# One opening stage for modulation, projections and rates, and a second queue for the first recurrent weights

## The chip, the cores and the metric

The kernel runs on one core of one Trainium2 chip. Its time is the device time of one execution in microseconds (us); less is better. The engines are named as in the profile: PE (TensorE matmul), PEld (its weight load), DVE (VectorE), ACT (ScalarE), POOL (GpSimd) and SP (SyncE, which here only issues transfers). SPq marks an instruction of SP's queue that issues a transfer.

## The reference

A transformer block with conditioned normalisation, a recurrent attention layer with fast weights, and a mixture of experts. The change touches the opening of it:

```
mod = (silu(c) @ wmod).reshape(16, 6, 1, 256)
sa, ca, ga, sb, cb, gb = (mod[:, j] for j in range(6))
ga, gb = (2 * (g >= 0) - 1) * max(abs(g), 0.25)
h   = layernorm(x) * (1 + ca) + sa              # x: (16, 256, 256)
qkv = silu(h @ W_qkv)                            # W_qkv: (256, 768); q and k scaled to length 1
lr  = softplus(h @ W_lr + b_lr + const)          # W_lr: (256, 6)
...                                              # recurrent stage over chunks of 64 tokens, w0, w1, w2
x = x + ga * attention
h = layernorm(x) * (1 + cb) + sb
x = x + gb * experts(h)                          # 64 experts, 6 for each token
```

## The kernel before

The program is a row of stages, each a block in which every engine has its own instruction list, with semaphores between them. A stage ends with a barrier of all engines (`PhaseSems.__exit__`, L65 and L66), before which SP waits for every store of the stage. The stages that matter here:

- `phase_modulation` (L118 to L187). SP loads `ct` (c transposed, 16 KB) and the whole of `wmod` (`wm`, 1536 KB). ACT and DVE make silu(c) out of Exp, add, reciprocal and multiply. PE makes all 1536 columns as 16 rows (a batch each), DVE copies them out of PSUM, adds 1 to the two scales and bounds the two gates, each step waiting for the one before. The table goes to DRAM (`scratch_mod`).
- `phase_qkv` (L190 to L450). 16 batches (b) of 256 tokens, two halves (u) of 128. A step s runs from -1 to 19; in it DVE has the statistics of batch s+1, ACT and PE the projection of batch s-1, DVE the lengths of q and k of batch s-2, PE and ACT the transposition of batch s-3 (`turn_y`, `keep_y`). `turn_h` transposes a normalised batch into `psH`; `keep_h` (ACT) copies it with the batch's scale and shift as per-partition operands, from `modT`, which is `scratch_mod` read back and transposed by PE. `qkv` makes 774 columns in `psQ`; `silu` (ACT) and `rates` (DVE, L393) empty it. `store_kv` and `store_t` write to DRAM, and so does a store of the 6 unfinished rates of each token (`scratch_zlr`). `psT` serves both `turn_y` and, ahead of the loop, the transposed modulation.
- `phase_rates` (L453 to L485). Reads `scratch_zlr` as 128 x 192, does softplus with Exp and Ln (another table of ACT), and writes `scratch_lr`.
- `phase_fast_weights` (from L560). The recurrent stage: two streams x of 16 iterations. PE and DVE both begin with `wait_ge(preload, 192)`, which is 12 loads of 128 KB: `firstT` (6, the weights transposed) and `first` (6). All are on SP's queue: `firstT`, then `load_kv(0, 0)` (4 of `kvT`, 2 of `kv`, 2 of `lr`), then `first`. Behind these stand `load_kv(1, 0)`, `wproj`, `onorm`, `wgate`. DVE, before its first piece of the recurrence, sums the squares of `firstT` (L1124, L1127), scales `wproj` (L1320), and adds to `code` (L1323), which POOL makes after the roots of those sums (L1346).
- The later stages (routing, experts, combination) read `scratch_mod` for the gate, at another index after the change, and are otherwise the same.

The order on each engine is the order of the code; nothing reorders it.

## Time and profile before

| | us |
|---|---|
| median of 3 runs | 1862.06 (1853.25 to 1863.24) |
| the profiled execution, its own time | 1872.18 |
| its span, first to last instruction | 1870.4 |
| PE busy | 1605.9 (86% of the span) |
| DVE busy | 1176.2 (63%) |
| ACT busy | 884.2 (47%) |
| POOL busy | 783.5 (42%) |
| modulation stage, to the first instruction of the next | 0 to 25.35 |
| projection stage | 25.35 to 164.51 |
| rates stage | 164.51 to 170.97 |

A busy share is a mean over the whole span. The stages follow each other with a barrier between them, so the time of a short stage is read from its own stretch of the trace, where the engines are mostly idle, and not from the shares.

### The profile page before, as it was taken

The page shows a single profiled execution, that of the slowest core. Times are in us where ns is not written, and L with a number is a line of the kernel's source. Part 1 is how long each engine was busy: PE and PEld are TensorE (multiplying, and loading weights), DVE is VectorE, ACT ScalarE, POOL GpSimd, SP SyncE. Part 2 cuts the span into 40 slices and gives each one's busy share as a digit, 9 for nine tenths or more (in the row PEclk, how much of TensorE's full clock was granted, in tenths as well). Part 3 has the DMA queues.
Part 4 walks back from the last instruction along what each step waited for, and adds up shares of the span by engine and source line. Part 5 has one row for each costly group of instructions (what it writes and reads, how often), then busy time and mean ns, then how long its engine had stood idle before and what let it go on. Part 6 is the DMA issues. An engine that isn't in the chain of part 4 may idle for free. (4 is left out here: it accounts for less than half of the span.)

```text
span 1870.4 us, 41123 instructions
## 1 busy us (share of the span) xinstructions
PE 1605.9 (86%) x11163; PEld 1197.3 (64%) x11227; DVE 1176.2 (63%) x4255; ACT 884.2 (47%) x2156; POOL 783.5 (42%) x818
## 2 busy tenths in 40 slices
PE   3993799888888888898872499999999999998996
PEld 1662577666666676666651377777777777776764
DVE  2662578878887778888873454444444444443877
ACT  1773377656566666666650133333333333332221
POOL 0331233455455545555567133333333333342333
PEclk7996799989998989999995699999999999999999
DMA  2675444444444442223223455555555556323997
GB/s 87 186 213 170 118 138 129 129 146 141 128 139 136 146 129 81 78 82 95 67 80 120 128 161 160 166 160 167 159 157 167 153 166 202 95 57 74 266 269 191
DMA packets 264288, 263.54 MB, mean 141 GB/s; under 512 B 87931, under 2 KB 235880, under 8 KB 264080
## 3 DMA queue, kind: packets, MB, share of 16 engines
q1 hardware_dynamic: 200592, 170.98, 32.1%
q0 software_dynamic: 21504, 51.18, 7.7%
q10 hardware_dynamic: 41984, 38.82, 7.6%
q8 instruction: 105, 1.72, 0.4%
q14 instruction: 103, 0.84, 0.2%
HBM read 141.91 MB, written 127.31 MB: 144 GB/s over the span
## 5 line engine op out<-in xcount | busy, mean ns | idle before, releaser
L1728 POOL DMA_INDIRECT scratch_y<-e_eo,e_goes x256 | 250.4, 978 | 408.8 <-ACT e_eo L1818 349.4
L1754 PE MATMUL e_psGU<-wgu,e_xT 128*128 x1024 | 352.1, 466 | 4.9 <-ACT e_xT L1811 2.7
L1862 DVE COPY e_hT<-e_psH 88x256 f32<-88x256 f32 x256 | 107.7, 421 | 338.3 <-PE e_psH L1763 257.5
L1770 PE MATMUL e_psD<-wd,e_hT 88*128 x1024 | 263.8, 380 | 0.0
L1754 PEld LDWEIGHTS e_psGU<-wgu,e_xT 128*128 128x128 f32 x1024 | 183.8, 190 | 92.6 <-issue 24.9
L1392 POOL DMA_INDIRECT scratch_buf<-rows,dest x192 | 192.0, 1000 | 49.1 <-issue 48.9
L1402 POOL TENSOR_TENSOR f_wnr<-f_wss,f_half 128x4 f32<-128x4 f32 x96 | 99.8, 1040 | 266.9 <-DVE f_wss L1212 265.0
L1807 ACT ACTIVATE e_sgm<-e_psGU 128x176 f32<-128x176 f32 x256 | 81.2, 317 | 239.5 <-PE e_psGU L1754 200.7
L1770 PEld LDWEIGHTS e_psD<-wd,e_hT 88*128 88x128 f32 x1024 | 174.1, 190 | 14.1 <-issue 0.4
L1818 ACT ACTIVATE e_eo<-e_psD 128x256 f32<-128x256 f32 x256 | 98.1, 383 | 159.0 <-issue 93.3
L1740 PEld LDWEIGHTS e_psX<-ident,e_xg 128*128 128x128 f32 x512 | 72.3, 141 | 73.1 <-issue 39.6
L1740 PE MATMUL e_psX<-ident,e_xg 128*128 128x128 f32 x512 | 98.3, 274 | 6.1 <-DMA e_xg<-scratch_buf 6.1
L1811 ACT ACTIVATE e_xT<-e_psX 128x256 f32<-128x256 f32 x256 | 97.2, 380 | 6.2 <-issue 5.7
L1048 ACT ACTIVATE f_wsq<-f_WT 128x512 f32<-128x512 f32 x96 | 60.5, 630 | 83.7 <-DVE f_WT L1208 76.6
L889 PE MATMUL prod<-f_A,f_beta_i 128*128 128x512 bf16 x192 | 74.8, 390 | 20.7 <-DVE f_A L1199 14.1
L891 PEld LDWEIGHTS prod<-f_A 128*128 128x128 bf16 x768 | 60.5, 100 | 47.9 <-issue 4.4
L1016 ACT ACTIVATE f_X<-spare 128x512 bf16<-128x512 f32 x96 | 57.4, 598 | 71.1 <-PE spare L908 71.1
L322 PE MATMUL q_psQ<-q_wq,q_hT 128*128 128x512 f32 (+1 forms) x256 | 90.5, 498 | 0.0
L1884 DVE TENSOR_TENSOR e_hh<-e_psGU,e_sgm 128x176 f32<-128x176 f32 x256 | 84.8, 331 | 5.7 <-ACT e_sgm L1807 5.6
L2051 DVE SCALAR_TENSOR_TENSOR c_acc<-c_g,wk,c_acc 128x256 f32<-128x256 f32 x160 | 78.6, 491 | 5.7
L1397 POOL TENSOR_TENSOR f_nb<-f_ssb,f_half 128x12 bf16<-128x12 bf16 x32 | 72.5, 2264 | 13.6 <-DVE f_ssb L1184 13.1
L891 PE MATMUL prod<-f_A 128*128 128x128 bf16 x768 | 76.0, 223 | 0.0
(305 smaller groups left out, 3779.3 us busy)
## 6 DMA issues: line engine op xcount, KB each, us to landing
e_xg<-scratch_buf ACTq DMA_DIRECT2D x256, 132.0 KB
scratch_y<-f_blank SPq DMA_DIRECT2D x64, 384.0 KB
c_g<-scratch_y SPq DMA_DIRECT2D x64, 384.0 KB, 12.0
scratch_qkvT<-q_tT SPq DMA_DIRECT2D x16, 768.0 KB
wgu<-in_wgT SPq DMA_DIRECT2D x64, 176.0 KB
wgu<-in_wuT SPq DMA_DIRECT2D x64, 176.0 KB
wd<-in_wdT SPq DMA_DIRECT2D x64, 176.0 KB
scratch_buf<-f_blank SPq DMA_DIRECT2D x65, 132.0 KB, 2.2
```

Source lines behind the costliest of these rows:

```text
L322: mm = pe.matmul(psQ[:, u, lo:hi], hT[:, b % 2, k, u, :], wq[:, k, lo:hi], start=(k == 0), stop=(k == KD - 1))
L891: mm = pe.matmul(dst[:, q, :], a[:, x, m, q, :], a[:, x, m, q, :], start=False, stop=(q == Q - 1))
L1392: pool.indirect_dma_start(out=T["buf"], out_offset=bass.IndirectOffsetOnAxis(dest[:, i, k:k + 1], 0), in_=rows[:, i % RR, :], in_offset=No ...
L1402: pool.tensor_tensor(wnr[:, x, cols], wss[:, x, cols], half[:, 0:Q], ALU.pow).then_inc(wn1[x].sem, 1)
L1728: pool.indirect_dma_start(out=T["y"], out_offset=bass.IndirectOffsetOnAxis(goes[:, n:n + 1], 0), in_=eo[:, n % OB, :], in_offset=None, bou ...
L1740: mm = pe.transpose(psX[:, j % 2, k * P:(k + 1) * P], xg[j % GB][:, k * P:(k + 1) * P], ident[:, :])
L1754: mm = pe.matmul(psGU[:, j % 2, 0:2 * F], xT[:, j % 2, k, :], wgu[:, bass.ds(buf, 1), k, :].rearrange("p b n -> p (b n)"), start=(k == 0), ...
L1770: mm = pe.matmul(psD[:, j % 2, 0:D], hT[0:FH, j % 2, k, :], wd[0:FH, buf, k, :].rearrange("p b n -> p (b n)"), start=(k == 0), stop=(k == 1))
L1811: act.activation(xT[:, j % 2, :, :].rearrange("p k t -> p (k t)"), psX[:, j % 2, 0:KD * P], ACT.Copy).then_inc(xd, 1)
L1818: act.activation(eo[:, b % OB, :], psD[:, b % 2, 0:D], ACT.Copy).then_inc(eod, 1)
L1862: v.tensor_copy(hT[0:FH, b, :, :].rearrange("p k t -> p (k t)"), psH[0:FH, b, 0:2 * P]).then_inc(htd, 1)
L1884: v.tensor_tensor(hh[:, b, :], psGU[:, b, F:2 * F], sgm[:, b, :], ALU.mult).then_inc(hd, 1)
```

## The change

Three things. First, `phase_modulation` and `phase_rates` are gone and their work stands in `phase_qkv`. The shift and scale of the first normalisation are made by PE directly as columns (`modT`, channels on partitions) from the first 512 columns of `wmod`; ACT's Silu makes silu(c). The other four rows are made after step 2 (`other_columns` on PE, `others` on DVE) in `psT`, which PE must not use again until DVE has copied it (`pe.wait_ge(n_kept, 1)`), and stored at step 4. Secondly, the rates stay in SBUF (`zl`, 128 x 32 x 6); softplus is done in the last steps, and `scratch_lr` has another layout: (128, 32, 6), so that a chunk's 64 tokens are 64 rows of 24 bytes, 768 bytes apart, where they were adjacent. The 16 stores of `scratch_zlr` are gone. Thirdly, in the recurrent stage the six loads of `first` are issued by ACT, and `firstT` stands on SP's queue behind `load_kv(0, 0)`.

```diff
-def phase_modulation(nc, T):
...
-def phase_rates(nc, T):
...
 def phase_qkv(nc, T):
@@ sync
-            load(0)
-            sp.dma_start(mod[:, :], T["mod"][:, 0:2, :].rearrange("b j d -> b (j d)")).then_inc(m_in, 16)
+            wv = T["wmod"].rearrange("(k p) n -> p k n", p=P)
+            sp.dma_start(ct[:, :].rearrange("p (k b) -> p k b", k=KD),
+                         T["cT"].rearrange("(k p) b -> p k b", p=P)).then_inc(c_in, 16)
+            load(0)
+            sp.dma_start(wm[:, :, 0:2 * D], wv[:, :, 0:2 * D]).then_inc(m_in, 16)
             sp.dma_start(wq[:, :, 0:3 * D], T["wqkv"].rearrange("(k p) n -> p k n", p=P)).then_inc(wload, 16)
             sp.dma_start(wq[:, :, 3 * D:NQ], T["wlr"].rearrange("(k p) n -> p k n", p=P)).then_inc(wload, 16)
+            load(1)
             sp.dma_start(blr[:, :], T["blr"].rearrange("(a n) -> a n", a=1).broadcast_to([P, NLR])).then_inc(wload, 16)
-            for b in range(1, NX):
+            load(2)
+            sp.dma_start(wm[:, :, 2 * D:6 * D], wv[:, :, 2 * D:6 * D]).then_inc(n_in, 16)
+            for b in range(3, NX):
                 load(b)
...
+            sp.wait_ge(lr_d, 1)
+            sp.dma_start(T["lr"].rearrange("p t n -> p (t n)"), lr[:, :, :].rearrange("p t n -> p (t n)")).then_inc(lr_out, 16)
@@ tensor
+            def other_columns():
+                pe.wait_ge(n_in, 16)
+                for n in range(2):
+                    for k in range(KD):
+                        mm = pe.matmul(psT[0:B, n * 512:(n + 1) * 512], ct[:, k * B:(k + 1) * B],
+                                       wm[:, k, 2 * D + n * 512:2 * D + (n + 1) * 512], start=(k == 0), stop=(k == KD - 1))
+                mm.then_inc(n_made, 1)
...
+            pe.wait_ge(c_silu, 1)
             pe.wait_ge(m_in, 16)
             for j in range(2 * KD):
-                mm = pe.transpose(psT[:, j * B:(j + 1) * B], mod[:, j * P:(j + 1) * P], ident[0:B, 0:B])
-            mm.then_inc(m_turned, 1)
-            pe.wait_ge(m_kept, 1)
-            pe.wait_ge(wload, 48)
+                for k in range(KD):
+                    mm = pe.matmul(psT[:, j * B:(j + 1) * B], wm[:, k, j * P:(j + 1) * P], ct[:, k * B:(k + 1) * B],
+                                   start=(k == 0), stop=(k == KD - 1))
+            mm.then_inc(m_made, 1)
+            pe.wait_ge(id_done, 2)
...
+                if s == 2:
+                    pe.wait_ge(m_kept, 2)
+                    other_columns()
+                    pe.wait_ge(n_kept, 1)
@@ scalar, after the halves of step s
+                if s == B:
+                    act.preload_act_table_set("natural_log_exp_and_others")
+                    act.wait_ge(neg_d, 1)
+                    act.activation(low[:, :, :], low[:, :, :], ACT.Exp).then_inc(exp_d, 1)
+                    act.wait_ge(exp_d, 1)
+                    act.activation(low[:, :, :], low[:, :, :], ACT.Ln, bias=1.0).then_inc(ln_d, 1)
@@ vector
-            v.wait_ge(wload, 48)
             for s in steps:
+                if s == 1:
+                    v.wait_ge(wload, 48)
                 if real(s - 2):
                     rates(s - 2, 1)
+                if s == B + 1:
+                    v.wait_ge(zl_d, B * UPB)
+                    v.scalar_tensor_tensor(out=low[:, :, :], in0=zl[:, :, :], scalar=-1.0, in1=zl[:, :, :],
+                                           op0=ALU.mult, op1=ALU.min).then_inc(neg_d, 1)
...
                 if real(s - 1):
                     rates(s - 1, 0)
+                if s == 2:
+                    others()
+            v.wait_ge(ln_d, 1)
+            v.scalar_tensor_tensor(out=lr[:, :, :], in0=zl[:, :, :], scalar=0.0, in1=low[:, :, :],
+                                   op0=ALU.max, op1=ALU.add).then_inc(lr_d, 1)
 def phase_fast_weights:
-        lrv = T["lr"].rearrange("(g x s c t) n -> x s g c t n", g=NG, x=2, s=2, c=NC)
+        lrv = T["lr"].rearrange("(h t) (g x s u) n -> x s g u h t n", t=CH, g=NG, x=2, s=2)
@@ sync
-            for w, n in enumerate(names):
-                for b2 in range(2):
-                    sp.dma_start(firstT[:, w, 2 * b2:2 * b2 + 2, :], T[n + "T"].rearrange("h p n -> p h n")).then_inc(preload, 16)
...
             load_kv(0, 0)
             for w, n in enumerate(names):
                 for b2 in range(2):
-                    sp.dma_start(first[:, w, 2 * b2:2 * b2 + 2, :], T[n].rearrange("h p n -> p h n")).then_inc(preload, 16)
+                    sp.dma_start(firstT[:, w, 2 * b2:2 * b2 + 2, :], T[n + "T"].rearrange("h p n -> p h n")).then_inc(preload, 16)
             load_kv(1, 0)
@@ scalar
+            for w, n in enumerate(names):
+                for b2 in range(2):
+                    act.dma_start(first[:, w, 2 * b2:2 * b2 + 2, :], T[n].rearrange("h p n -> p h n")).then_inc(preload, 16)
             act.preload_act_table_set(ACT_SET)
```

`others` does to the four rows on DVE what `phase_modulation` did to six: the copy out of PSUM (16 x 1024 where it was 16 x 1536), the added 1 (one row now), and the six steps of the gates on 16 x 512, each waiting for the one before.

How the lists move at three places. SP's list from the start of the program, before:

```order
L142 DMA m_ct<-in_cT 128x2x16
L144 DMA m_wm<-in_wmod 128x2x1536
L146 DMA scratch_mod<-m_mod 16x1536
L120 UNCONDITIONAL_BRANCH
L244 UNCONDITIONAL_BRANCH
L249 DMA q_x<-in_x 128x2x256
L266 DMA q_mod<-scratch_mod 16x512
L267 DMA q_wq<-in_wqkv 128x2x768
L268 DMA q_wq<-in_wlr 128x2x6
L269 DMA q_blr<-in_blr 128x6
```

and of the change:

```order
L198 DMA q_ct<-in_cT 128x2x16
L184 DMA q_x<-in_x 128x2x256
L201 DMA q_wm<-in_wmod 128x2x512
L202 DMA q_wq<-in_wqkv 128x2x768
L203 DMA q_wq<-in_wlr 128x2x6
L184 DMA q_x<-in_x 128x2x256
L205 DMA q_blr<-in_blr 128x6
L184 DMA q_x<-in_x 128x2x256
L207 DMA q_wm<-in_wmod 128x2x1024
```

The store of the table, the barrier (the two branches) and the read back are gone; the second batch of x stands between the two small loads, behind 512 KB of `wm` and 768 KB of `wq`.

PE's list at the end of step 2 and in step 3, of the change (before, the same without the row of L277):

```order
L269 MATMUL q_psQ<-q_wq,q_hT 128x262 x2
L277 MATMUL q_psT<-q_wm,q_ct 16x512 x4
L251 MATMUL q_psH<-q_ident,q_xn 128x128 x4
L258 MATMUL q_psT<-q_ident,q_y 128x128 x6
L269 MATMUL q_psQ<-q_wq,q_hT 128x512 x2
L269 MATMUL q_psQ<-q_wq,q_hT 128x262 x2
```

Four matmuls of 512 columns stand between the last projection of batch 1 and `turn_h(3)`, and `turn_h(3)` also waits for DVE's copy.

ACT's list at the end of the projections, of the change (before, the four `keep_y` of the row L317 follow the square at once, and the table load, Exp and Ln stand behind a barrier):

```order
L331 ACTIVATE q_sq<-q_y 128x512
L351 ACT_TABLE_LOAD
L353 ACTIVATE q_low<-q_low 128x192
L355 ACTIVATE q_low<-q_low 128x192
L317 ACTIVATE q_tT<-q_psT 128x6x128 x4
L123 UNCONDITIONAL_BRANCH
L972 UNCONDITIONAL_BRANCH
L1073 DMA f_first<-in_w 128x2x128 x6
L1074 ACT_TABLE_LOAD
```

The softplus moved ahead of the last four copies, and ACT begins the recurrent stage with six issues.

## Rows read from the trace of the kernel before

**Rows 1.** The page, part 1: busy us, share, instructions.

```profile
PE 1605.9 (86%) x11163; PEld 1197.3 (64%) x11227; DVE 1176.2 (63%) x4255; ACT 884.2 (47%) x2156; POOL 783.5 (42%) x818
```

**Rows 2.** Busy time by stretch: engines, granted clock, DMA share, GB/s.

```profile
0.00:25.35 25.35, 7.27 (x12) 1.31 (x12) 5.91 (x11) 1.51 (x2) 0.20 (x4) 0.90 0.23 67
25.35:39.55 14.20, 2.58 (x13) 2.13 (x14) 4.59 (x19) 2.53 (x4) 2.01 (x6) 0.50 0.56 169
60.00:150.00 90.00, 90.00 (x415) 60.58 (x414) 58.91 (x181) 66.54 (x102) 28.52 (x24) 1.00 0.72 218
164.51:170.97 6.46, 0.00 (x0) 0.00 (x0) 0.72 (x2) 2.01 (x3) 0.00 (x0) 0.50 0.10 30
170.97:194.97 24.00, 2.83 (x24) 2.46 (x24) 7.90 (x18) 1.67 (x2) 7.65 (x25) 0.57 0.51 135
173.00:175.00 2.00, 0.00 (x0) 0.00 (x0) 0.00 (x0) 0.00 (x0) 1.56 (x6) 0.50 0.85 234
```

**Rows 3.** DMA issues, 0 to 25 us: KB each, us to landing.

```profile
m_ct<-in_cT SPq DMA_DIRECT2D x1, 16.0 KB, 1.9
```

**Rows 4.** Order of time, modulation stage: start, us, engine, line, operation.

```profile
0.79 0.45 SPq L142 DMA_DIRECT2D m_ct<-in_cT  x1
...
8.28 0.23 ACT L152 ACTIVATE m_ec<-m_ct 128x32 f32<-128x32 f32 x1 [6.21 <-DMA m_wm<-in_wmod]
...
16.77 1.75 DVE L177 COPY m_mod<-psM 16x1536 f32<-16x1536 f32 x1 [7.44 <-PE psM L159]
...
21.51 0.68 DVE L186 TENSOR_TENSOR m_mod<-m_sgn,m_mag 16x512 f32<-16x512 f32 x1
```

**Rows 5.** Order of time, start of the projection stage.

```profile
33.11 0.75 DVE L406 BATCH_NORM_STATS2 q_stats<-q_x 128x6 f32<-128x256 f32 x2 [10.92 <-DMA q_blr<-in_blr]
...
35.86 0.75 DVE L406 BATCH_NORM_STATS2 q_stats<-q_x 128x6 f32<-128x256 f32 x2
...
39.55 7.61 PE L322 MATMUL q_psQ<-q_wq,q_hT 128*128 128x512 f32 x16
```

**Rows 6.** Order of time, steps 2 and 3 of the projection stage.

```profile
47.43 5.37 PE L322 MATMUL q_psQ<-q_wq,q_hT 128*128 128x512 f32 x16
...
52.63 0.62 PE L306 MATMUL q_psH<-q_ident,q_xn 128*128 128x128 f32 x4
...
53.66 0.23 DVE L393 SCALAR_TENSOR_TENSOR q_zl<-q_psQ,q_blr 128x6 f32<-128x6 f32 x2
...
57.49 0.73 DVE L426 TENSOR_SCALAR q_xn<-q_x,q_aggr,q_rstd 128x256 f32<-128x256 f32 x2 [0.25 <-POOL q_rstd L296]
...
59.90 0.27 PE L306 MATMUL q_psH<-q_ident,q_xn 128*128 128x128 f32 x1
```

**Rows 7.** Order of time, end of the projection stage and the rates.

```profile
151.41 0.79 ACT L357 ACTIVATE q_tT<-q_psT 128x768 f32<-128x768 f32 x1
...
155.18 0.88 PE L313 MATMUL q_psT<-q_ident,q_y 128*128 128x128 f32 x6 [1.98 <-DVE q_y L432]
...
158.59 0.81 ACT L357 ACTIVATE q_tT<-q_psT 128x768 f32<-128x768 f32 x1 [1.69 <-PE q_psT L313]
...
164.51 1.28 ACT L481 ACT_TABLE_LOAD   x1 [5.11 <-PEq L66]
```

**Rows 8.** Order of time, start of the recurrent stage.

```profile
178.47 3.15 SPq L755 DMA_DIRECT2D f_first<-in_w  x6
...
184.00 1.90 DVE L1124 TENSOR_TENSOR f_wsq<-f_firstT 128x512 f32<-128x512 f32 x3 [12.74 <-DMA f_first<-in_w]
...
187.89 2.28 POOL L1346 TENSOR_TENSOR f_wn<-f_wss,f_half 128x12 f32<-128x12 f32 x1 [12.53 <-DVE f_wss L1127]
...
192.12 0.26 DVE L1323 TENSOR_SCALAR f_code<-f_code,f_later 128x32 f32<-128x32 f32 x1 [0.98 <-POOL f_code L1365]
```

**Rows 9.** Order of time: iteration 1 of stream 0, load and first use.

```profile
200.13 1.91 SPq L710 DMA_DIRECT2D f_kvT<-scratch_qkvT  x4
...
226.29 1.12 PE L801 MATMUL prod<-f_Wn,f_kvT 128*64 128x128 f32 x8
```

More of the change, by code:

```diff
@@ L225, in phase_qkv @@
         psT = ps("psT", [P, 1024])
-        wload, id_done, consts, m_in, m_turned, m_kept = (sems.take("q_" + n) for n in (
-            "wload", "ident", "consts", "m_in", "m_turned", "m_kept"))
+        wload, id_done, consts, c_in, m_in, n_in, c_silu, m_made, m_kept, n_made, n_kept, n_out = (sems.take("q_" + n) for n in (
+            "wload", "ident", "consts", "c_in", "m_in", "n_in", "c_silu", "m_made", "m_kept", "n_made", "n_kept", "n_out"))
+        neg_d, exp_d, ln_d, lr_d, lr_out = (sems.take("q_" + n) for n in ("neg", "exp", "ln", "lr", "lr_out"))
         x_in = [sems.take(f"q_x_in{i}") for i in range(NX)]
@@ L256, in store_kv @@
                              y[:, b % NY, :, D:3 * D]).then_inc(kv_out[b % NY], 16)
-                sp.dma_start(T["zlr"][rows, :].rearrange("(u p) n -> p u n", p=P),
-                             zl[:, b % NY, :, :]).then_inc(kv_out[b % NY], 16)
             def store_t(b):
@@ L278, in _ @@
                     store_t(s - 3)
+                if s == 4:
+                    sp.wait_ge(n_kept, 8)
+                    sp.dma_start(T["mod"].rearrange("b j d -> b (j d)"), mod[:, :, :].rearrange("b j d -> b (j d)")).then_inc(n_out, 16)
+            sp.wait_ge(lr_d, 1)
+            sp.dma_start(T["lr"].rearrange("p t n -> p (t n)"), lr[:, :, :].rearrange("p t n -> p (t n)")).then_inc(lr_out, 16)
+            sp.wait_ge(n_out, 16)
+            sp.wait_ge(lr_out, 16)
             for i in range(NY):
-                sp.wait_ge(kv_out[i], 32 * len(range(i, B, NY)))
+                sp.wait_ge(kv_out[i], 16 * len(range(i, B, NY)))
             for i in range(2):
@@ L319, in qkv @@
                     pe.wait_ge(zl_d, (b - 1) * UPB + u + 1)
+                if b == 0 and u == 0:
+                    pe.wait_ge(wload, 48)
                 for lo, hi in ((0, 512), (512, NQ)):
@@ L2081, in scratch_shapes @@
 def scratch_shapes():
-    return {"mod": (B, 6, D), "kv": (N, 2 * D), "lr": (N, NLR), "zlr": (N, NLR), "qkvT": (3 * H, HD, N),
+    return {"mod": (B, 4, D), "kv": (N, 2 * D), "lr": (P, TT, NLR), "qkvT": (3 * H, HD, N),
             "xh": (TT // 2, P, 2, 2, D), "buf": (BUF_ROWS, ROW), "y": (N * TOPK, D)}
 def program(nc, T):
-    phase_modulation(nc, T)
     phase_qkv(nc, T)
-    phase_rates(nc, T)
     with ExitStack() as ctx:
```

137 lines of the change are left out of this document (37 added, 100 removed).

## The prediction

> **What bounds the kernel now.** I read the page first. PE is busy for 1605.9 us, 86% of the span [rows 1], which looks like a kernel that only faster matmuls can help. Next I cut the span into its stages with the table by stretches [rows 2]. The reader is to see there that the mean hides the opening. In the first 25.35 us PE works for 7.27 us. From 25.35 to 39.55, where the first projection starts, it works for 2.58. From 164.51 to 170.97, the rates, it does nothing. From 170.97 to 194.97 it works 2.83 of 24.00. These stretches are latency: a transfer, a short chain of engines, a barrier. Only the middle of the projection stage is full: 90.00 of 90.00 us on PE at the full granted clock, with DVE at 58.91 and ACT at 66.54. Whatever the change puts on PE, or makes PE wait for, in that middle costs its whole length. Then I read the order of time through each opening, and the row of the first transfer's landing [rows 3 to 8]. Nothing before 195 us runs beside the later stages, so a microsecond gained here should be one gained at the end.
>
> **1. The start of the program.** Before, the first projection matmul starts at 39.55 [rows 5]. I work out when it starts now. SP's first issue is at 0.79, and the first small transfer lands 1.9 us later [rows 3, 4]. `ct` and `wmod`, 1552 KB, had landed at 8.28, 7.49 us after the first issue [rows 4]; less 1.9 us for a landing that is 5.6 us, 277 KB per us. Batch 1 of x stands now behind 16 + 256 + 512 + 768 + 6 KB and is 256 KB itself: 1814 KB, 6.5 us of transfer, with 1.9 for landing 8.4. Small rows cost more than their bytes: in the projection stage 1065 KB (x, the table of 16 partitions, `wq`, and the two loads with rows of 24 bytes) took from 25.35 to 33.11, 7.76 us, where 277 KB per us and a landing give 5.7. So 2.0 us went to three awkward transfers. Of these one (`wlr`) now stands ahead of batch 1: 0.7. Batch 1 lands at 0.79 + 8.4 + 0.7 = 9.9. Bounds: no surcharge, 9.2; all of it, 11.2.
>
> From the statistics of batch 1 to the first projection took 39.55 - 35.86 = 3.7 us [rows 5], through DVE, POOL, DVE again and `turn_h(1)`. The same chain follows now, so the first projection starts at 13.6. Two other paths must be shorter. Batch 0 and the 512 KB of `wm` land at about 5 and at 0.79 + 784/277 + 1.9 = 5.5; eight matmuls with 16 columns each I bound by the four-instruction groups of this stretch, 2.58 us of PE for 13 instructions [rows 2], so 1.6 us, to 3 us if each takes twice that; two ACT copies and `turn_h(0)` with its copies, another 3: ready at 10 to 11.5. The last piece of `wload` is 3 KB behind batch 1: about 10.7. Both are before 13.6. The gain is 39.55 - 13.6 = 26.0, bounds 24.5 and 27.
>
> This includes the modulation's whole tail (the copy, the gate chain, the store, a barrier, the read back), which no longer stands ahead of anything.
>
> **2. The other four rows, in the middle.** Four matmuls of 512 columns by 16 rows: eight of 512 and eight of 262 take 5.37 us in step 2 [rows 6], so 0.43 for one of 512 columns if time goes by columns, 1.7 for four. PE then waits for DVE's copy of 16 x 1024: 1.75 us for 1536 columns [rows 4], so 1.2, and 0.1 for the handover. DVE is free by then: its `rates(1, 0)` is at 53.66 in the old trace [rows 6], 1.0 after PE's last matmul of step 2, and now PE has 1.7 us more to do. A wait that the old step 3 had for `xn` falls inside: -0.1. Sum 1.7 + 1.3 = 3.0.
>
> Behind the copy DVE runs seven more steps. The old chain from the copy's start to the end took 21.51 + 0.68 - 16.77 = 5.42 us, 1.75 of it the copy [rows 4]; one row less in the first step takes 0.15 off the rest: 3.5. What is queued behind it on DVE is `rates(1, 1)` and then all of step 3: the sums, the statistics of batch 4, its `xn`. In the old trace `rates(1, 1)` starts 1.0 after `turn_h(3)`, and `xn` starts 57.49 - 53.66 = 3.8 after it [rows 6]. Now, with `turn_h(3)` as zero, the copy ends at about -0.1, the chain at 3.5, `xn` for batch 4 starts at 7.3 and is done at 8.0. PE would want it at 59.90 - 52.63 = 7.3. A stall of 0.7, and some 0.3 for the lengths behind it (`scale_qk`, `rates(2, 0)`). After that DVE, with a third of each period free [rows 2], is back in its place within a step. So this part costs 3.0 + 1.0 = 4.0. Bounds: 3.0, if the stall is absorbed, and 6.5, if each of seven waits costs DVE 0.3 more in a stage where it has other waits.
>
> **3. The end of the stage.** On ACT a table load (1.28 [rows 7]), Exp and Ln of 128 x 192 (2.01 us of ACT in the rates stretch with the table load and its third instruction [rows 2], so 0.36 each) now stand before `keep_y(14, 0)`, at 151.41 before. It slips by 2.1. PE's next transposition waits for it, ACT copies, and `turn_y(15, 0)`, at 155.18 because DVE's scaled q and k came then [rows 7], now starts at 156.3, after two slipped copies (0.8 each) and one transposition (0.9). 1.0 of the slip was covered by DVE's chain; 1.1 is left, and 0.2 for a colder clock in the gaps. The last `keep_y` moves by 1.3. If that cover were gone the slip would be 2.1.
>
> The Trainium skill (ScalarE: Activation LUTs, "What ACT_TABLE_LOAD costs") gives a load of 1283 ns and a drain of 1380 ns with it, 2.66 us for a switch; the load agrees with the 1.28 of the row, and no row here shows the drain, since ACT was idle around every load. By the page the slip would be 1.4 us more, and the sum that much worse.
>
> The store of `lr` (96 KB) is one issue and a quarter of a us of transfer behind the last store of `qkvT`: 0.3. Against these 1.6 stands the rates stage, 6.46 us from barrier to barrier [rows 2], all gone. Gain 4.9, bounds 3.3 (table slip 2.9) and 6.0.
>
> The 16 stores of `zlr` leave SP's queue, but PE has no gap there to give back: nothing.
>
> **4. The first weights of the recurrent stage.** Everything waits for 12 loads, until 184.00, 13.03 us after the stage began at 170.97 [rows 2, 8]. The last issue ended at 181.62 and landed 2.4 later. Now SP's six issues of `firstT` (3.1 us by the 3.15 for `first` [rows 8]) stand behind only `load_kv`: SP ends them 3.1 us sooner. That needs the transfers to keep up: 2048 KB by the wait in 10 us. In 173 to 175 the engines moved 234 GB/s at a busy share of 0.85 [rows 2], 275 at full: 7.4 us of pure work, starting some 1.2 us into the stage, plus the landing, ends at 10 or 11. So the two limits are nearly equal, and I take 2.7 for the gain, bounds 1.3 and 3.1.
>
> What is late next: DVE's sums (3.8 us), POOL's roots at 187.89 and then its tables, until DVE's 192.12 [rows 8]. All of these follow the wait, or `wgate`, which is also issued 3.1 sooner. So the 2.7 is handed on.
>
> The Trainium skill (DMA: Bandwidth & Descriptors, "Issuing engines are not separate DMA queues") says that transfers of all issuing engines share the same 16 DMA engines, and that a second issuer saves only issue time. The share of 0.85 with one issuer agrees. Taken strictly, as the rival below has it, this part gives nothing.
>
> **The sum.** -26.0 + 4.0 - 4.9 - 2.7 = -29.6. The profiled execution took 1872.18 us, 1.8 more than its span; it would take 1843. The median of the runs, 1862.06, lies 10.1 below that execution, in a stretch that the change doesn't touch as far as I can tell, so the forecast is 1862.06 - 29.6 = 1832.5.
>
> **The rivals.**
>
> *The transfers are slower than I have them.* The start now hangs on one queue with 1.8 MB ahead of batch 1, and `preload` on two queues that share the engines. For it: DMA is busy only 0.23 and 0.56 of the old openings [rows 2], so no row shows 3 MB streamed at once. Against it: 1552 KB did stream at 277 KB per us. Batch 1 at 13.2, 2 us past my bound, costs 3.3, and part 4 its 2.7, so with the rest as forecast 1838.5.
>
> *DVE doesn't catch up.* PE has no slack in the middle, and DVE's chain through POOL sets `xn`. If the lag of step 3 lasted into steps 4 and 5 at 1 to 2 us each: 1835.5. The 90.00 of 90.00 on PE with DVE at 58.91 speaks against it.
>
> *Slower than before: the scattered rates.* `lr` rows lie 768 bytes apart now, and `load_kv`'s eight transfers are waited for together, 32 times. To lose the 29.6 us and 9.3 more it would have to add 1.2 us in each of 32 loads to the chain. But stream 0's load for iteration 1 is issued from 200.13 and first used at 226.29 [rows 9]: the two small loads would have to land some 20 us late before they cost anything. It decides only from there: at 22 us of landing, 1871.
>
> *The change does its work but the stretch was not on the path.* The barriers exclude it: nothing of a later stage starts before the one ahead is done. It would give 1862.
>
> **How the numbers follow.** The forecast, within its parts' bounds (their sum runs from -24.5+6.5-3.3-1.3 = -22.6 to -27+3-6-3.1 = -33.1, so 1829 to 1839.5), 0.75. The slower transfers beyond these bounds 0.08; DVE's lag beyond them 0.04; a gain beyond 1829 (a clock on PE that rises sooner, since the first projections ran at 0.50) 0.07; the scattered rates, or another loss that eats it all, 0.03; no gain 0.03. The runs of before spread over 10 us by themselves, so the range is 1824 to 1842. A measurement tells about 0.5%, 9.3 us: faster than 1852.8 0.94, within 0.03, slower 0.03.
>
> **What would show it.** In the profile after one sees the first projection matmul at 13.6 (12.5 to 15) and DVE's second statistics at 9.9; four matmuls of L277 at about 27 and 1.3 us of idle PE behind them, then another idle of about 0.7 at `turn_h(4)`; `keep_y` behind Ln, and the last copy about 1.3 later against the last square; the recurrent stage's wait ends 10.3 us after its start, at about 184.00 - 29.6 = 154.4 in the trace. The prediction is wrong if batch 1 lands late, if PE's idle in the middle exceeds 5 us, or if the time from 195 us on, which I take as unchanged, moves by more than the runs' own spread.

## The result, and the profile after

The kernel after took 1841.83 us (median of 4 runs, 1835.83 to 1845.6), the kernel before beside it 1862.65 (4 runs, 1853.25 to 1867.43): 20.8 us less, a ratio of 0.9892 [0.9863, 0.9922]. It is faster, by 1.1%. The forecast was 1832.5, 29.6 us less, a ratio of 0.984, which lies outside the interval of the ratio; the median lies at the upper end of the range given. The profiled execution took 1845.60, 26.6 less than the profiled one of before.

The page of the kernel after, its first row and its line of the granted clock:

```profile
PE 1626.9 (88%) x11235; PEld 1210.5 (66%) x11235; DVE 1176.6 (64%) x4252; ACT 883.9 (48%) x2156; POOL 785.2 (43%) x818
PEclk9995999989898899999965799999999999998999
```

Against [rows 1] PE has 21 us more of busy time in a kernel that is faster: the sum of the shares says nothing here, as it said nothing before. The stretches do. The columns are those of [rows 2]:

```profile
0.00:13.32 13.32, 5.41 (x25) 5.04 (x25) 4.68 (x19) 2.82 (x6) 2.22 (x10) 1.00 0.78 264
20.27:30.92 10.65, 9.34 (x30) 3.97 (x28) 6.01 (x17) 5.23 (x8) 2.30 (x2) 1.00 0.23 74
133.00:140.50 7.50, 4.54 (x18) 3.43 (x18) 1.94 (x5) 2.42 (x5) 0.80 (x1) 0.50 0.54 189
146.40:157.39 10.99, 0.00 (x0) 0.00 (x0) 0.22 (x3) 1.28 (x1) 3.73 (x12) 0.50 0.83 210
```

The columns are: start and end, length, busy time of PE, PEld, DVE, ACT and POOL with their instructions, granted clock, DMA share, GB/s. The first stretch replaces 39.55 us: the DMA engines are now busy for 0.78 of it, where they were at 0.23 and 0.56. The second is step 2 with the four rows, the third the transpositions of the last batch, at half the clock, and the fourth the wait for the first weights.

**The start**, in order of time:

```profile
4.11 0.75 DVE L374 BATCH_NORM_STATS2 q_stats<-q_x 128x6 f32<-128x256 f32 x2 [4.11 <-DMA q_x<-in_x]
6.00 3.57 PE L285 MATMUL q_psT<-q_ct,q_wm 128*128 128x16 f32 x16 [6.00 <-DMA q_wm<-in_wmod]
9.63 0.75 DVE L374 BATCH_NORM_STATS2 q_stats<-q_x 128x6 f32<-128x256 f32 x2 [2.67 <-DMA q_x<-in_x]
12.41 1.12 PE L251 MATMUL q_psH<-q_ident,q_xn 128*128 128x128 f32 x4 [1.91 <-DVE q_xn L394]
13.32 1.06 PE L269 MATMUL q_psQ<-q_wq,q_hT 128*128 128x512 f32 x1
```

Batch 1 of x is there at 9.63 (forecast 9.9), the first projection starts at 13.32 (forecast 13.6). The bracket at 12.41 says what it waited for: the statistics chain of batch 1, and not the modulation, which PE ended at 9.57. The projection's first record takes 1.06 and the next ones stand 0.85 apart until 16.7, twice the 0.43 of step 2: they ran at the lower level of the clock, though the profile's clock column gives 1.00 for this stretch.

**The four rows in step 2, and step 3:**

```profile
20.27 0.60 PE L251 MATMUL q_psH<-q_ident,q_xn 128*128 128x128 f32 x4
20.71 5.37 PE L269 MATMUL q_psQ<-q_wq,q_hT 128*128 128x512 f32 x16
26.00 3.61 PE L277 MATMUL q_psT<-q_wm,q_ct 128*16 128x512 f32 x8
29.65 1.21 DVE L411 COPY q_mod<-q_psT 16x1024 f32<-16x1024 f32 x1 [2.56 <-PE q_psT L277]
30.92 0.66 PE L251 MATMUL q_psH<-q_ident,q_xn 128*128 128x128 f32 x4 [1.31 <-DVE q_mod L411]
33.72 0.68 DVE L419 TENSOR_TENSOR q_mod<-q_sgn,q_mag 16x512 f32<-16x512 f32 x1
39.00 0.66 PE L251 MATMUL q_psH<-q_ident,q_xn 128*128 128x128 f32 x4 [0.91 <-DVE q_xn L394]
```

The code has four matmuls at L277 and the trace eight records, each 0.43 us: 3.61 us where I had 1.7. (The transpositions show one record for each call: four at L251 for four calls, six at L258 for six.) The next two numbers are near those of the forecast: PE idle for 1.31 behind DVE's copy, and for 0.91 at `turn_h(4)` (forecast 0.7).

**The end of the stage:**

```profile
130.33 0.63 ACT L331 ACTIVATE q_sq<-q_y 128x512 f32<-128x512 f32 x1
130.98 1.28 ACT L351 ACT_TABLE_LOAD   x1
132.28 0.36 ACT L353 ACTIVATE q_low<-q_low 128x192 f32<-128x192 f32 x1
132.94 0.79 ACT L317 ACTIVATE q_tT<-q_psT 128x768 f32<-128x768 f32 x1
133.88 1.51 PE L258 MATMUL q_psT<-q_ident,q_y 128*128 128x128 f32 x6 [3.77 <-ACT q_tT L317]
136.38 1.51 PE L258 MATMUL q_psT<-q_ident,q_y 128*128 128x128 f32 x6 [0.99 <-ACT q_tT L317]
138.89 1.51 PE L258 MATMUL q_psT<-q_ident,q_y 128*128 128x128 f32 x6 [0.99 <-ACT q_tT L317]
140.44 0.81 ACT L317 ACTIVATE q_tT<-q_psT 128x768 f32<-128x768 f32 x1 [1.69 <-PE q_psT L258]
141.68 0.54 SPq L221 DMA_DIRECT2D scratch_lr<-q_lr  x1
```

The first of the last four copies starts 2.61 us behind the square, where it was 0.53 behind it: the slip of 2.1 that I worked out. What I didn't see is what PE does meanwhile: it sits idle for 3.77 us, the granted clock is at the lower of its two levels (1.2 GHz, 0.50 in the row above), and all three transpositions take 1.51. Before, the first two of them took 0.85 and 0.88 [rows 7] and only the last 1.51; the square and these two in the trace of before:

```profile
150.88 0.63 ACT L371 ACTIVATE q_sq<-q_y 128x512 f32<-128x512 f32 x1
152.35 0.85 PE L313 MATMUL q_psT<-q_ident,q_y 128*128 128x128 f32 x6 [1.70 <-ACT q_tT L357]
157.04 1.51 PE L313 MATMUL q_psT<-q_ident,q_y 128*128 128x128 f32 x6 [0.99 <-ACT q_tT L357]
```

The last copy ends 5.15 us before the next stage starts (5.11 before): the store of `lr` costs 0.04.

**The start of the recurrent stage**, at 146.40:

```profile
146.41 3.48 ACTq L1073 DMA_DIRECT2D f_first<-in_w  x6
153.71 0.97 SPq L714 DMA_DIRECT2D f_firstT<-in_w1T  x2
157.39 1.90 DVE L1086 TENSOR_TENSOR f_wsq<-f_firstT 128x512 f32<-128x512 f32 x3 [10.70 <-DMA f_firstT<-in_w1T]
165.50 0.26 DVE L1285 TENSOR_SCALAR f_code<-f_code,f_later 128x32 f32<-128x32 f32 x1 [0.99 <-POOL f_code L1327]
```

The wait is 10.99 us (13.03 before). It ends with `firstT`, whose last issue on SP is over at 154.68. So the last issue that everything waits for ends 8.28 us into the stage where it ended 10.65 into it, 2.4 sooner, and lands 2.71 later where it was 2.38. From the wait's end to the last of DVE's preparations, 8.11 us pass, as in [rows 8] (8.12).

### The profile page after: what moved, and what is told of

It is laid out like the page before. It is cut to its first block and busy times, and to the rows that moved or that the text cites. A ratio compares the mean times of both kernels' runs of the same rounds, so it can differ in the third digit from the quotient of the medians.

```text
span 1843.5 us, 41093 instructions
## 1 busy us (share of the span) xinstructions
PE 1626.9 (88%) x11235; PEld 1210.5 (66%) x11235; DVE 1176.6 (64%) x4252; ACT 883.9 (48%) x2156; POOL 785.2 (43%) x818
## 5 line engine op out<-in xcount | busy, mean ns | idle before, releaser
L847 PE MATMUL prod<-f_gamma_r,f_gamma_l 128*128 128x512 bf16 x192 | 76.3, 397 | 8.7 <-DVE f_A L1161 5.5
```

## The experiments

The kernels ran in three sets: the first four in one where the kernel before took 1823.29, the next four in one where it took 1870.72, the last two in one where it took 1822.12. The record gives chip number 1 for the first two sets and 8 for the third, so it doesn't show whether the level of a set belongs to the chip. Each kernel is compared with the runs of before in its own set, and the openings are compared in the traces. Theory A, in all that follows: the opening is 26.6 us shorter, no later stage is touched, and what the medians show beside it is the variation of the later stages. The rival, Theory B: part of the gain is given back behind 195 us, for which the scattered rates are the candidate.

### Both kernels again

No edit.

> The changed kernel, nothing edited, with five rounds against the kernel before. The two profiled executions differ by 26.6 us, the medians of four runs each by 20.8. Theory A: the opening gives 26.6 us in every execution, and the runs of the later stages, which differ from one execution to the next, hid 6 us of it; then this profile shows the recurrent stage's wait ending at 157.4 again within 0.3 us, and the ratio tends to 0.986. Theory B: something after the opening gives back about 6 us in the changed kernel; then the ratio stays near 0.989, with an interval that leaves out 0.986, and the stretch behind 168 us is longer in this trace than the 1675.5 us of the kernel before. Chances 0.65 and 0.35.

> The kernel before, nothing edited, for a second profile on the chip of the others. Theory A (executions differ in the later stages only): the wait of the recurrent stage ends at 184.0 within 0.3 us, the span differs from 1870.4 by some us (about 1860 by the median of the runs), and the difference lies behind 195 us. Rival: the opening itself varies by several us, and then no trace of one execution can carry a sum in tenths.

The kernel after took 1795.05 (6 runs, 1786.64 to 1797.71), before 1823.29 (9 runs): 0.9845 [0.9825, 0.9865], 28.2 us less. In the traces the first projection starts at 12.51 against 38.70, the wait for the first weights ends at 156.84 against 182.78, so 25.9 us earlier. That start is 0.8 earlier than in the first trace and the end of the wait 0.55 earlier, where 0.3 was allowed; the points of before moved by 0.9 to 1.2 us. The interval leaves out the 0.989 of Theory B.

> The changed kernel once more, unchanged, for the one thing that the first two sets of runs leave apart: the medians differed by 20.8 us (1862.65 against 1841.83) and by 28.2 us (1823.29 against 1795.05). Theory A: the openings are 26.6 us shorter in every profile, the later stages are untouched and only vary with the granted clock from one execution to the next, so the difference of medians is 26.6 with the runs' own spread on it: a ratio of 0.984 to 0.987, and f_code within 1 us of 165.5 in the profile. Theory B: part of it is given back after 195 us on a chip whose recurrent stage is slow, and not on the faster chip: 0.989 again if the kernel before is above 1850 us here, 0.9845 if it is below 1830.

This time 1797.15 (5 runs) against 1822.12 (9 runs): 0.9858 [0.9833, 0.9883], 25.0 us less. That is in Theory A's range; its second number is missed by a hair (the last preparation at 166.53, 1.03 later). The kernel before was below 1830 here, the case in which B expects 0.9845, and the interval holds both numbers: this run doesn't separate the theories. B's case above 1850 was not met by the kernel after; the second set, below, meets it with `all_late`.

What the later stages do shows in one stretch, from the first to the last scatter of rows (POOL, the routing part of the recurrent stage), here the kernel after in its first profile and in that of `after_again`:

```profile
333.20:998.60 665.40, 559.43 (x5452) 430.40 (x5451) 525.45 (x1647) 399.01 (x918) 386.04 (x371) 0.91 0.36 114
331.70:949.30 617.60, 522.77 (x5452) 398.63 (x5452) 521.80 (x1647) 393.28 (x918) 386.01 (x371) 0.96 0.39 123
```

The same counts of work, 665.4 us against 617.6, at a granted clock of 0.91 and 0.96. The kernel before has nearly the same two lengths: 666.7 in the trace of [rows 1] and 618.9 in `before_again`. So this stretch differs by 48 us from one set to another, whichever kernel runs. For all twelve profiles, the opening (to the start of the addition to `code`, 192.12 in [rows 8]) and what is left to the last instruction:

| | opening | the rest | span |
|---|---|---|---|
| before | 192.12 | 1678.3 | 1870.4 |
| after | 165.50 | 1678.0 | 1843.5 |
| before_again | 191.10 | 1631.4 | 1822.5 |
| after_again | 164.93 | 1619.7 | 1784.6 |
| one_queue | 168.91 | 1625.6 | 1794.5 |
| chain_late | 164.90 | 1625.0 | 1789.9 |
| rows_late | 160.07 | 1689.5 | 1849.6 |
| soft_later | 164.66 | 1678.3 | 1843.0 |
| weights_ahead | 160.80 | 1681.9 | 1842.7 |
| all_late | 152.70 | 1678.6 | 1831.3 |
| after_third | 166.53 | 1628.5 | 1795.0 |
| all_late_again | 153.34 | 1630.8 | 1784.1 |

The rest varies by 11 to 12 us among the four executions of the first set and among those of the second. So that it is the same to 0.3 us in the first pair is a coincidence of two executions. A cost of the scattered rates, which every kernel from `after` on has, would be in it, and none shows: with the kernel before it is 1678.3 and 1631.4, the latter the longest of its set. A cost below this variation is not excluded, and no run takes the layout of the rates back by itself.

### Where the middle's time went: the chain, and the rows

`chain_late` leaves the four matmuls and the copy where they are, and moves the seven steps on DVE to the end of the stage (shortened, the comments say what the function holds):

```diff
@@ vector
                 if s == 2:
-                    others()          # copy and seven steps
+                    others()          # the copy alone
...
+            gate_steps()              # the seven steps
             v.wait_ge(ln_d, 1)
@@ sync
-                if s == 4:
-                    sp.wait_ge(n_kept, 8)
-                    sp.dma_start(T["mod"]...)
...
+            sp.wait_ge(n_kept, 8)
+            sp.dma_start(T["mod"]...)
             sp.wait_ge(lr_d, 1)
```

> The changed kernel with the seven steps of the four rows behind DVE's copy moved to the end of the stage, and their store too; the matmuls, the copy and PE's wait for it stay after step 2. Theory A: the copy and the four matmuls cost PE 4.5 us (turn_h(3) 4.5 late against the first projection) and the chain on DVE 0.8 more at turn_h(4); then turn_h(3) stays at 30.9 and turn_h(4) comes at 37.9 to 38.2 where it was 39.0, and the last copy of the stage is about 1 us earlier. Rival: DVE was late anyway, turn_h(4) stays within 0.3 of 39.0.

PE in order of time, `turn_h(3)` and the two that follow it, and the first transposition of the tail:

```profile
31.74 0.66 PE L250 MATMUL q_psH<-q_ident,q_xn 128*128 128x128 f32 x4 [1.31 <-DVE q_mod L410]
38.75 0.60 PE L250 MATMUL q_psH<-q_ident,q_xn 128*128 128x128 f32 x4
45.71 0.60 PE L250 MATMUL q_psH<-q_ident,q_xn 128*128 128x128 f32 x4
133.28 0.84 PE L257 MATMUL q_psT<-q_ident,q_y 128*128 128x128 f32 x6 [3.77 <-ACT q_tT L316]
```

The idle time behind the copy is the same 1.31; the two steps after it take 7.01 and 6.96, where they took 8.08 and 7.30 in the kernel after. So the chain costs 1.4 us, in two steps, and DVE has caught up after them. `turn_h(4)` itself is at 38.75 and not at the 37.9 to 38.2 expected, since the step before the rows was 0.8 longer here. The last copy of the stage is 1.27 earlier, and this is not the 1.4 alone: the longer first step takes 0.8 off, and one transposition at the full clock gives 0.7. For the idle time of PE in the tail is 3.77 here as in the kernel after, and yet the first transposition behind it took 0.84 (the other two 1.52 and 1.51). The wait for the first weights ends 0.83 earlier than in the first trace of the kernel after and 0.28 earlier than in `after_again`, which ran in the same set. Its one execution took 1791.97.

Three lengths of the projection stage, from the traces: from the first projection to `turn_h(2)`, from there to the last square, and from the last square to the recurrent stage (before the change with the 6.46 of the rates in it):

| | to `turn_h(2)` | to the last square | to the next stage |
|---|---|---|---|
| before | 7.44 | 103.89 | 20.09 |
| before_again | 7.36 | 103.88 | 20.04 |
| after | 6.95 | 110.06 | 16.07 |
| after_again | 7.48 | 110.05 | 16.06 |
| chain_late | 7.73 | 108.63 | 16.12 |
| rows_late | 6.14 | 103.88 | 17.21 |
| soft_later | 7.04 | 110.05 | 14.73 |
| all_late | 6.82 | 103.88 | 14.83 |
| all_late_again | 6.95 | 103.89 | 14.83 |

The second length repeats to 0.01 us, so the rows cost 6.2 us in the middle. The first has the same work in all of them and changes with how long PE stays at the lower clock.

`rows_late` takes the matmuls out of step 2 as well. They go, one pair for each half, into step 17, where PE waits for the last lengths, and write to `psH`, which is free by then:

```diff
@@ tensor
-                if s == 2:
-                    pe.wait_ge(m_kept, 2)
-                    other_columns()
-                    pe.wait_ge(n_kept, 1)
...
                     if real(s - 1):
                         qkv(s - 1, u)
+                    if s == B + 1:
+                        other_columns(u)      # one pair of the four, into psH
@@ vector
-                if s == 2:
-                    others()
+            others()
             v.wait_ge(ln_d, 1)
```

> The changed kernel with the four rows made in the last steps instead of after step 2: PE's matmuls in two pairs after the two transpositions of batch 14, written to psH, which nobody reads any more, so that PE waits for no copy; DVE's copy and seven steps after its last scaling, and the store behind them. Theory A: the 5.3 us that turn_h(4) is late against the first projection are all due to the rows; then turn_h(4) comes at 33.5 to 33.8, and the recurrent stage begins 4 to 6 us sooner than at 146.4, the less the two pairs (1.7 us each) cover PE's idle time there. If the clock fell at the end only for want of work on PE, the transpositions of batch 15 take 0.85 each instead of 1.51. Rival: the tail takes them in worse than the middle, the stage begins at 144 or later.

`turn_h(3)` follows `turn_h(2)` by 5.64 us, exactly as before the change (52.63 in [rows 6], less the 46.99 below), and 10.65 in the kernel after. The price of the middle is gone: all 6.2 us of it. `turn_h(4)` comes at 32.30 (33.5 to 33.8 expected), 0.8 of it by the shorter first step. The next stage begins at 140.48 instead of 146.40. `turn_h(2)` of before, and the tail of `rows_late` (PE, with DVE's copy):

```profile
46.99 0.60 PE L306 MATMUL q_psH<-q_ident,q_xn 128*128 128x128 f32 x4
126.82 0.84 PE L257 MATMUL q_psT<-q_ident,q_y 128*128 128x128 f32 x6 [1.95 <-ACT q_tT L315]
127.60 3.46 PE L276 MATMUL q_psH<-q_wm,q_ct 128*16 128x512 f32 x4
131.09 1.21 DVE L409 COPY q_mod<-q_psH 16x1024 f32<-16x1024 f32 x1 [2.58 <-PE q_psH L276]
132.93 0.85 PE L257 MATMUL q_psT<-q_ident,q_y 128*128 128x128 f32 x6 [0.99 <-ACT q_tT L315]
```

The second pair fell into a stretch at the lower clock and took 3.46 for four records, twice the 1.8 of the middle; of the two transpositions behind it the first took 0.95 and the second 0.85, the full clock again. The tail as a whole is 1.1 longer than in the kernel after (17.21 against 16.07). The opening ends at 160.07, 5.4 less than after. Its one execution took 1851.63, the longest of the four of its set: with a rest of 1689.5, 8 to 11 us above the others of that set, a single execution cannot show 5 us.

### The end of the stage

```diff
@@ scalar, after the halves of step s
-                if s == B:
+                if s == B + 1:
                     act.preload_act_table_set("natural_log_exp_and_others")
```

> The changed kernel with the table load, Exp and Ln one step later on ACT, after the two copies of batch 14; nothing else. In the kernel before ACT idles 2.0 us there. Theory A: the softplus ahead of the copies cost 2.4 us at the last copy (1.1 by ACT itself, the rest because PE, left without work for 3.8 us, did three transpositions at the low clock); then the last copy comes at about 138.0 to 138.6 where it was 140.4, and the recurrent stage begins 1.5 to 2.4 us sooner. Theory B: a table load has a drain of 1.4 us with it, which shows here behind a running engine: the gap between the copy ahead of it and Exp is 2.7 us or more.

```profile
132.01 0.85 PE L258 MATMUL q_psT<-q_ident,q_y 128*128 128x128 f32 x6 [1.70 <-ACT q_tT L317]
132.90 0.81 ACT L317 ACTIVATE q_tT<-q_psT 128x768 f32<-128x768 f32 x1 [1.03 <-PE q_psT L258]
133.72 1.28 ACT L351 ACT_TABLE_LOAD   x1
135.02 0.36 ACT L353 ACTIVATE q_low<-q_low 128x192 f32<-128x192 f32 x1
135.23 1.54 PE L258 MATMUL q_psT<-q_ident,q_y 128*128 128x128 f32 x6 [2.37 <-DVE q_y L400]
```

The last square was at 130.54; the next stage begins 14.73 behind it, 16.07 in the kernel after: 1.3 less, just under the 1.5 to 2.4 expected, and the last copy is at 139.31 (138.0 to 138.6 expected). The slip of the copies is gone, and one of three transpositions has the full clock back. The other two have not: PE still waits 2.37 for DVE. Against before 1.06 is left at the last copy: 0.66 for one transposition more at the lower clock, 0.4 because DVE's own part of the softplus (`low`, 0.36) stands ahead of its last sums. Its one execution took 1845.15.

Here the table load also follows an ACT instruction with no gap, which no row of before had: the copy ends at 133.71, the load begins at 133.72, Exp 0.02 behind its end, at 135.02. In the kernel after it is 130.98 + 1.28 to 132.28, the same. The Trainium skill (ScalarE: Activation LUTs, "What ACT_TABLE_LOAD costs") has another 1.38 us of drain in each switch; neither trace has it.

### The first weights

```diff
@@ scalar
-            for w, n in enumerate(names):
-                for b2 in range(2):
-                    act.dma_start(first[...]...)
@@ sync, behind firstT
+            for w, n in enumerate(names):
+                for b2 in range(2):
+                    sp.dma_start(first[...]...)
```

> The changed kernel with the six loads of first back on SP's queue, behind firstT; nothing else. The wait took 11.0 us in the changed kernel and 13.0 in the one before. Theory A, two issuers save issue time: SP has 12 issues and load_kv again, 4.5 + 6.2 + 2.4 for the landing, so the wait ends 13.0 us after the stage begins, 2.0 more than with two. Theory B, the 16 DMA engines are the limit and a second issuer gives nothing: the wait stays at 11.0 to 11.5, and the 2 us came from the order (load_kv first).

From the stage's begin to the end of the wait (columns as in [rows 2]), and the last issues:

```profile
146.64:160.70 14.06, 0.00 (x0) 0.00 (x0) 0.22 (x2) 1.28 (x1) 3.72 (x12) 0.50 0.63 164
154.90 3.04 SPq L717 DMA_DIRECT2D f_first<-in_w  x6
```

14.06 us where 13.0 was expected. Two issuers against one are worth 3.1 in the new order (14.06 against 10.99; 10.74 in the same set, 3.3). But with one issuer the new kernel is 1.0 slower than before (13.03; 12.80 in the same set, 1.3). SP has the same 20 issues ahead of the wait in both; they take 11.30 us instead of 10.65, 0.4 of it in a gap between the second and the third issue of `firstT` that before hasn't, and the last one lands after 2.76 instead of 2.38. Whether this comes from the order or from the scattered rows of `lr` was not separated. The DMA engines are busy for 0.63 of the stretch with one issuer and for 0.83 with two (0.91 in `after_again`). The Trainium skill (DMA: Bandwidth & Descriptors, "Issuing engines are not separate DMA queues") says that a second issuer saves only the time of issuing, usually small. The runs agree with the first half; here that time, 3.04 for six issues, was a fifth of the wait of 14.06.

`weights_ahead` takes the twelve loads out of the wait: SP issues them in steps 6 to 8 of the projection stage, into tensors that outlive it, and waits for them before that stage's end.

```diff
@@ phase_qkv, sync
+                if 6 <= s < 9:
+                    n = ("w0", "w2", "w1")[s - 6]
+                    for dst, src in ((first, n), (firstT, n + "T")):
+                        for b2 in range(2):
+                            sp.dma_start(dst[:, s - 6, 2 * b2:2 * b2 + 2, :], T[src]...).then_inc(pre, 16)
@@ phase_fast_weights
-            pe.wait_ge(preload, 192)
-            v.wait_ge(preload, 192)
```

> The changed kernel with all 12 loads of first and firstT issued by SP in steps 6 to 8 of the projections, into memory that both stages keep; SP waits for them at the stage's end. Nothing waits for them in the recurrent stage. Theory A: the wait of 11.0 us is the 12 loads; then PE's first matmul waits for load_kv alone, 4.5 us of issue and 2.4 of landing, and starts 6.5 to 7 us after the stage begins; DVE starts its squares at once, and the first scaled piece (the row of f_sg) comes not 19.3 us after the begin but 12 to 14, bounded by wgate and by POOL's tables. The projection stage pays less than 1 us. Rival: the loads crowd out the stores there and the projections take it back, 3 us or more.

The middle of the projections, and the opening of the recurrent stage, which begins at 147.32:

```profile
50.00:110.00 60.00, 60.00 (x277) 40.52 (x276) 41.37 (x131) 44.16 (x69) 20.35 (x18) 1.00 0.79 246
153.85 1.97 PE L762 MATMUL prod<-first,f_kvT 128*64 128x128 f32 x16 [12.53 <-DMA f_lr<-scratch_lr]
160.27 0.61 DVE L1279 TENSOR_SCALAR f_wproj<-f_wproj,f_onorm 128x256 f32<-128x256 f32 x2 [8.59 <-DMA f_wgate<-in_gateT]
```

PE loses nothing to the loads: 60.00 of 60.00, with the DMA share at 0.79 (0.68 in the kernel after). The stage still begins 0.9 later than in the kernel after, 0.8 of it in the stretch up to `turn_h(2)` (7.73), ahead of these loads. The opening of the recurrent stage is 5.6 us shorter (13.48 from its begin to `code`, 19.10 in the kernel after). It is not the 11 of the wait, because the loads behind it are late next: PE waits 6.5 us for `kvT`, `kv` and `lr`, and DVE 8.59 for `wgate`, the last small load on SP's queue. Its one execution took 1844.5.

### All of it together

`all_late` is `rows_late`, `soft_later` and `weights_ahead` in one kernel. It leaves out nothing of the computation.

> The three edits together: four rows in the last steps, softplus one step later, the first weights loaded during the projections. Theory: each acts on another wait, so their gains add: 4 to 6, 1.5 to 2.4 and 5 to 7 us, less some us where the rows and the softplus meet in the same tail; the span shortens by 10 to 14 us against the changed kernel, and the ratio to the kernel before is 0.980 to 0.984. Rival: later stages give part of it back as they may have for the change itself, ratio 0.985 or above.

```profile
123.82 1.89 PE L283 MATMUL q_psH<-q_wm,q_ct 128*16 128x512 f32 x4
130.67 0.85 PE L264 MATMUL q_psT<-q_ident,q_y 128*128 128x128 f32 x6 [0.99 <-ACT q_tT L322]
131.55 0.81 ACT L322 ACTIVATE q_tT<-q_psT 128x768 f32<-128x768 f32 x1 [1.03 <-PE q_psT L264]
```

Both pairs of matmuls are at the full clock now (1.89 for the second, 3.46 in `rows_late`), and so are the three transpositions of the tail (0.87, 0.87, 0.85). The last copy comes 7.43 behind the last square (124.12), where it was 7.71 before the change, 10.11 after it. Not all of that reaches the next stage: it begins 14.83 behind the square, 14.73 in `soft_later`, most likely because the two stores that now stand last (`mod` and `lr`) are issued at 134.04 and 134.44, behind DVE's chain; no run tests this. So the four matmuls cost 0.1 here in the tail, where they cost 1.1 in `rows_late`. The opening ends at 152.70: 12.8 less than after, more than the 11.0 of the three edits one by one (5.4, 0.8 and 4.7). The tail accounts for 1.0 of the difference; the remaining 0.8 lies within what the opening of the unedited kernel after moves by itself, 164.93 to 166.53. It took 1833.71 (6 runs), 0.9793 [0.9749, 0.9837] of before, just past the 0.980 expected. That is 37.0 us less, of 39.4 in the openings, in the set where before took 1870.72: against Theory B.

> The combination once more beside the kernel after, on one chip, to compare the two directly. It leaves out no part of the computation. Its opening was 12.8 us shorter than that of the kernel after (152.70 against 165.50), so Theory A expects its median 12.8 us below the other's, between 10 and 15 with the spread. Theory B, in which what is won early is partly given back behind 195 us, expects 5 to 10.

1785.88 (5 runs, 1781.58 to 1787.86): 0.9785 [0.9766, 0.9804] of before, and 11.3 below the kernel after in the same set, whose runs (1793.56 to 1804.71) all lie above it. It is faster than both. Of 13.2 us in the openings of this set 11.3 arrive at the end, within the 10 to 15 of Theory A.

## Why the prediction was wrong, point by point

| us | forecast | measured in the traces |
|---|---|---|
| start, to the first projection | -26.0 | -26.2 |
| the four rows in the middle, to the last square | +4.0 | +5.7 |
| end of the stage, with the rates | -4.9 | -4.0 |
| first weights | -2.7 | -2.0 |
| sum | -29.6 | -26.6 |

1. **The start** was right, and so was what covers it: the chain of batch 1. The one doubtful term in it, the eight small matmuls at 1.6 to 3 us, took 3.57, above its bound: it was priced by transpositions, which show one record each, and the eight matmuls show 16 (point 2). It stayed covered: the copies of batch 0 that follow it end at 11.62, 1.7 before the first projection.

2. **The middle** is the step that failed. The mechanism was right in each of its parts: 1.31 for the copy (1.3 forecast), 0.81 and 0.35 for the chain (0.7 and 0.3), by which steps 3 and 4 are longer than before, and DVE back in place after two steps; `chain_late` gives back 1.4. The mis-sized term is "0.43 for one of 512 columns if time goes by columns, 1.7 for four": 3.61. I took the 16 records of [rows 6] for 16 matmuls. The code behind them, two halves by two ranges of columns by two k, has 8, and each shows as two records. The Trainium skill (FP8 and Floating Point Precision, "TensorE Precision Notes") states four passes for a true float32 product; with one column for each cycle, which that section does not state, a matmul of 512 columns at 2.4 GHz would be estimated at 512 x 4 / 2.4 = 853 ns, and the trace has 0.87 us for two records. A count of the calls in the code against the x of the row would have found the error. With the rows at their true price the middle costs 6.2, and the 5.7 of the table owes 0.5 to luck: the stretch up to `turn_h(2)` was 0.49 shorter than before in this pair and 0.12 longer in the second, where the same sum gives 6.3. Two slips of 0.1 in the prediction's sum go opposite ways: 5.37 us by columns is 0.44 for one of 512, not 0.43, and the -0.1 for `xn` was named and not taken.

3. **The end.** The step that I named, "1.1 is left, and 0.2 for a colder clock in the gaps", is the second that was mis-sized: 2.4 in place of 1.3, for the clock. PE, idle for 3.77 us, was at the lower level behind it, and two transpositions more than before took 0.65 longer each, on the path: 1.1 + 1.3. `soft_later` recovers 1.3 and shows that the softplus alone isn't all of it: behind PE's wait of 2.37 for DVE two of them are still at the lower clock. `all_late`, with matmuls in the gap, has all of them at the full clock. The term is not a fixed one: `chain_late` had the same 3.77 of idle time and only two at the lower clock. The store of `lr` cost 0.04 and not 0.3.

4. **The first weights.** A gain of 2.04 where "the two limits are nearly equal, and I take 2.7". The step that was off is "SP ends them 3.1 us sooner": it ended them 2.4 sooner, and the landing took 0.3 more. `one_queue` separates two things that I had netted without seeing them: the second issuer gives 3.1, and the new kernel with one issuer is 1.0 slower than before. The rival, that the second queue gives nothing, is out; it also went further than what the prediction takes from the Trainium skill, by which the time of issuing is saved.

5. **What was handed on.** Everything, in the first pair of traces: 8.11 us from the end of the wait, as before, and the same 1678 us behind it. None of the signs that the prediction names for being wrong appeared in the traces. A gain off the path is excluded by every comparison; a cost of the scattered rates showed in none.

6. **From 26.6 to 20.8.** Of the 8.8 us between forecast and measurement 3.0 are the rows of the table; 5.8 are in no trace. The openings' 26.6 would be a ratio of 0.9857, just outside the first interval [0.9863, 0.9922]. Three other comparisons lie within 2.4 us of their openings: 28.2 against 26.2, 37.0 against 39.4 (the first trace of before), 11.3 against 13.2; for the 25.0 there is no profile of before in its set. The most likely reason for the 5.8 is the rest, which varies by 11 to 12 us between executions, with four runs on each side; that is argued, and the cause of this part stays open.

## What to carry to other kernels

Before a duration of one record is used as that of one instruction, count the calls in the code that the row's x stands for. When work is moved, look for the place where its engine idles, and not only for one where the data is ready: the same four matmuls and what hangs on them cost 6.2 us in the middle of a full engine, and at the end 1.1, or 0.1 once the softplus was out of their way, where the transpositions behind them ran at the full clock. A price read from one execution can hold luck of the clock: take it between two points that repeat from trace to trace. When a wait for loads is taken away, the loads that were queued behind it are the next wait, so its length is no measure of the gain.

## What the runs showed of the hardware

- A float32 matmul of 512 columns is two records of 0.43 us at the full granted clock (3.61 for four matmuls) and about twice that at the lower one (3.46 for two). A float32 transposition of 128 x 128 is one record.
- The six-record transpositions took 0.82 to 0.88 us at the full clock and 1.51 at the lower one. Behind 3.77 us of idle TensorE all three were at the lower one in the kernel after, and only the last two in `chain_late`, with the same idle time. Behind gaps of 1.70, 1.98 and 0.99 they took 0.85, 0.88 and 1.51 (before). With matmuls in the gaps they took 0.87, 0.87 and 0.85 (`all_late`).
- The profile's clock column can read 1.00 where the records say otherwise: from the first projection to `turn_h(2)` it gives 1.00 in `after`, `chain_late` and `rows_late`, which took 6.95, 7.73 and 6.14 us for the same work, and the first records of it stood 0.85 apart instead of 0.43.
- An activation table load took 1.28 us, and the next instruction began 0.02 behind it, in two kernels.
- A second issuing engine raised the busy share of the DMA engines from 0.63 to 0.83 (0.91 in a second execution) over twelve loads of 128 KB and what goes with them.
- The same stretch of the same work took 665 us in one set of runs and 618 in another, at a granted clock of 0.91 and 0.96. Whether the clock is the whole cause was not examined.
